# A gated delta stage whose gate factors move from VectorE to ScalarE, and a routed stage whose blank rows are written in long pieces

## The reference, cut to what matters

```python
def step(S, inp):                       # layer 0, once per token; 16 heads of 64x64
    qt, kt, vt, at, bt = inp
    err = jnp.einsum('bhij,bhj->bhi', S, kt) - vt
    S = at[..., None] * S - bt[..., None, None] * (err[..., None] * kt[:, :, None, :])
    o = jnp.einsum('bhij,bhj->bhi', S, qt)
    return (S, o)
...
logits = (xf @ Wr + br) / TAU           # layer 3, routed experts
top_val, top_idx = jax.lax.top_k(logits, 2)
h = jnp.einsum('nd,edh->enh', xf, We1) + be1[:, None, :]
```

## Time and profile before

| | us |
|---|---|
| median of 3 runs (lowest, highest) | 3070.89 (3068.77, 3072.56) |
| the profiled execution, its own time | 3057.68 |
| its span | 3055.9 |
| busy in the span: PE, DVE, ACT, POOL | 2376.6, 2214.9, 1278.8, 272.4 |
| granted TensorE clock, mean share of full speed | 0.857 |

### The profile page before, as it was taken

One profiled execution on the slowest core, in us unless ns is written; L12 is line 12 of the kernel. 1 busy time (PEld: TensorE's weight loads), 2 busy tenths in 40 slices (PEclk: granted clock), 3 DMA queues, 4 the chain that ended last, 5 costly groups with the idle time before them and its releaser, 6 DMA issues. The chain is left out here.

```text
span 3055.9 us, 65022 instructions
## 1 busy us (share of the span) xinstructions
PE 2376.6 (78%) x25365; PEld 1619.7 (53%) x25365; DVE 2214.9 (72%) x4056; ACT 1278.8 (42%) x2862; POOL 272.4 (9%) x280
## 2 busy tenths in 40 slices
PE   6677777777777777769947999999767766778677
PEld 5667666666666666643314666666322221222366
DVE  6999999999999999960034877777255657665465
ACT  3333333333333333332225777776411132556334
POOL 0000000000000000000031010100022311110242
PEclk9777787877777878789977999999978887999888
DMA  4111101111111111011018999995000001110421
GB/s 173 30 30 30 30 22 24 30 30 30 30 30 30 30 30 30 16 39 27 0 50 228 250 229 244 234 239 137 35 0 0 0 23 56 41 41 24 156 68 62
DMA packets 200028, 214.43 MB, mean 70 GB/s; under 512 B 32150, under 2 KB 185766, under 8 KB 194310
## 3 DMA queue, kind: packets, MB, share of 16 engines
q1 hardware_dynamic: 197353, 205.39, 25.7%
q0 software_dynamic: 2400, 4.95, 0.5%
HBM read 138.16 MB, written 74.74 MB: 70 GB/s over the span
## 5 line engine op out<-in xcount | busy, mean ns | idle before, releaser
L1274 DVE TENSOR_REDUCE ra_top<-ps 128x1 f32<-128x512 f32 x256 | 161.6, 684 | 96.0 <-PE ps L1078 95.7
L2557 DVE TENSOR_REDUCE dl_ZO<-dl_XP 128x64 f32<-128x128 f32 (+6 forms) x448 | 219.7, 490 | 15.4
L2553 DVE TENSOR_TENSOR dl_XP<-dl_ZO,dl_G 128x64 f32<-128x64 f32 (+6 forms) x448 | 194.6, 434 | 15.4
L1928 DVE TENSOR_TENSOR ps<-ps,da_window 128x192 f32<-128x192 f32 (+1 forms) x256 | 101.3, 396 | 122.3 <-PE ps L1657 117.9
L1772 ACT ACTIVATE da_AB<-ps 128x384 f32<-128x384 f32 x256 | 124.8, 492 | 146.9 <-PE ps L1634 143.2
L1195 ACT ACTIVATE ra_PT<-ps 128x512 f32<-128x512 f32 x256 | 137.0, 597 | 115.6 <-PE ps L1097 115.5
L1782 ACT ACTIVATE da_E<-ps,da_top 128x512 f32<-128x512 f32 x256 | 176.3, 688 | 17.3 <-DVE da_top L1931 16.9
L1931 DVE TENSOR_REDUCE da_top<-ps 128x1 f32<-128x512 f32 x256 | 177.0, 691 | 8.8
L1664 PE MATMUL ps<-ident,da_E 128*128 128x128 f32 x1024 | 169.0, 288 | 1.3 <-ACT da_E L1782 1.2
L1473 POOL MEMSET da_K<- 32x4096 f32 x2 | 7.1, 3574 | 1559.8 <-POOLq L82 1559.8
L2163 PE MATMUL ps<-X,dl_taps_q 128*128 (+1 forms) x1088 | 144.8, 299 | 0.0
(11 more groups left out here) (397 smaller groups left out, 5668.2 us busy)
## 6 DMA issues: line engine op xcount, KB each, us to landing
da_bands<-da_AB SPq DMA_DIRECT2D x128, 384.0 KB, 3.8
dl_Abc<-dl_ends SPq DMA_DIRECT2D x64, 512.0 KB, 6.2
da_window<-da_bands SPq DMA_DIRECT2D x128, 192.0 KB, 4.4
da_across<-da_bands SPq DMA_DIRECT2D x128, 192.0 KB, 4.5
da_parts<-da_split SPq DMA_DIRECT2D x64, 96.0 KB, 3.4
rf_We<-in_rf_We SPq DMA_DIRECT2D x1, 4608.0 KB, 23.2
da_K<-da_parts SPq DMA_DIRECT2D x16, 256.0 KB
da_Q<-da_parts SPq DMA_DIRECT2D x16, 256.0 KB
```

Source lines behind the costliest of these rows:

```text
L1274: eng.tensor_reduce(top[:, m % 2, u:u + 1], ps[:, score_bank(UNITS * m + u), :], AXX, ALU.max, negate=True).then_inc(s["maxima"], 1)
L2553: link(eng.tensor_tensor(XP[:, :, :, SB - t:], seen.unsqueeze(1).to_broadcast([P, 2, I, t + 1]), G[:, x:x + 2, keys][:, ::-1, :].unsqueeze ...
L2557: link(eng.tensor_reduce(ZO[:, to:to + 1 + (2 * I - 1) * CH:CH].rearrange("p (k i) -> p k i", k=2), XP[:, :, :, SB - 1 - t:], AXX, ALU.add))
```

## The change

In the delta stage DVE now turns gates and values densely into the two halves of `dl_Y` (named `decays` and `values`), for all but the first pass. ACT copies the gates from there into `dl_aT` (512 columns), copies the half's 16 columns of `beta` and of minus `beta` into `dl_beta_now`, and writes `dl_bv` token by token: 16 activations of 32 columns, each scaled by its column of `beta_now`. When DVE has scanned `dl_F`, ACT writes `dl_FB` in the same way, 16 activations more. DVE's two products per half are gone. A new semaphore `laid` counts ACT's four steps per half; DVE's scan waits for the first, and `begin`, which overwrites `dl_Y`, for the last. In the second half `dl_FB` comes behind `later_products` on ACT. The first pass keeps the old way (`prepare_first`).

In the routed stage the fill of `rf_slots` is the same 2.8 MB, seen as 128 rows of 5590 floats in place of 5504 rows of 130, and the bias columns are laid out on the host with the experts side by side, so that the view in line 712 has step one.

```diff
-        yield [..., (s["filled"], [(slots, d["rf_blank"])]), (s["experts_loaded"], large)]
+        yield [..., (s["filled"], [(slots.rearrange("(p j) x -> p (j x)", p=P), d["rf_blank"].rearrange("(p j) x -> p (j x)", p=P))]), (s["experts_loaded"], large)]
...
-            own_bias = bias[:, 0:E * 2 * HR].rearrange("p (e m) -> p m e", e=E)
+            own_bias = bias[:, 0:E * 2 * HR].rearrange("p (m e) -> p m e", e=E)
...
+        values, decays = Y[:, 0:CH, :], Y[:, CH:, :]
...
+            def lay_out(m, e):
+                at = 2 * m + e + 1
+                eng.wait_ge(s["transposed"], 3 * at - 2)
+                eng.activation(aT[:, e, :, :, 1:].rearrange("p i u t -> p u t i"), decays[:, :, :].rearrange("p (u t) i -> p u t i", t=SB), ACT.Copy)\
+                   .then_inc(s["laid"], 1)
+                for sign in range(2):
+                    eng.activation(beta_now[:, sign, :], half_of(beta, m, e), ACT.Copy, scale=1.0 - 2.0 * sign).then_inc(s["laid"], 1)
+                eng.wait_ge(s["transposed"], 3 * at - 1)
+                eng.wait_ge(s["laid"], 4 * at - 9)
+                for t in range(CH):
+                    ins = eng.activation(bv[:, e, :, t], values[:, t, :], ACT.Copy, scale=beta_now[:, 0, t:t + 1])
+                ins.then_inc(s["laid"], 1)
+
+            def scale_decays(m, e):
+                at = 2 * m + e + 1
+                eng.wait_ge(s["transposed"], 3 * at)
+                for t in range(CH):
+                    ins = eng.activation(FB[:, e, :, t // SB, t % SB], F[:, e, :, t // SB, t % SB], ACT.Copy, scale=beta_now[:, 1, t:t + 1])
+                ins.then_inc(s["prep"], 1)
...
                 boundary(n, 0)
+                lay_out(n + 1, 0)
+                scale_decays(n + 1, 0)
                 evacuate(n + 1, AV, 6)
...
                 boundary(n, 1)
+                lay_out(n + 1, 1)
                 later_products(n + 1)
+                scale_decays(n + 1, 1)
...
+                eng.transpose(decays[:, :, :], aN[:, span, :]).then_inc(s["transposed"], 1)
+                eng.transpose(values[:, :, :], vN[:, span, :]).then_inc(s["transposed"], 1)
...
+            def prepare(m, e):
+                eng.wait_ge(s["laid"], 4 * (2 * m + e + 1) - 11)
+                accumulate(m, e)
...
             def begin(n, e):
                 j = 2 * n + e
                 at = BEGUN * j
+                eng.wait_ge(s["laid"], 4 * j)
                 eng.wait_ge(s["y"], 6 * j + 4)
```

More of the change, by code:

```diff
@@ L451, in routed_ffn @@
         ps = c.ps
-        yield [(s["loaded"], pairs), (s["filled"], [(slots, d["rf_blank"])]), (s["experts_loaded"], large)]
+        yield [(s["loaded"], pairs), (s["filled"], [(slots.rearrange("(p j) x -> p (j x)", p=P), d["rf_blank"].rearrange("(p j) x -> p (j x)", p=P))]), (s["experts_loaded"], large)]
         block = c.block(ctx)
@@ L2045, in delta_attention @@
              "gate", "var", "log", "scaled", "normed", "wo", "wo_copied", "transposed", "prefix", "prep", "whole",
-             "abc", "begun", "halves")
+             "abc", "begun", "halves", "laid")
     s = {n: c.nc.alloc_semaphore(name="dl_" + n) for n in names}
@@ L2078, in delta_attention @@
         bv = c.sb("dl_bv", [P, 2, I, CH], ctx)
+        beta_now = c.sb("dl_beta_now", [P, 2, CH], ctx)
         Y = c.sb("dl_Y", [P, XC, I], ctx)
+        values, decays = Y[:, 0:CH, :], Y[:, CH:, :]
         XP = c.sb("dl_XP", [P, 2, I, SB + 1], ctx)
@@ L2466, in turn_values, with accumulate, prepare_first @@
                 eng.wait_ge(s["evac"], m * PROJ + AV)
+                eng.transpose(decays[:, :, :], aN[:, span, :]).then_inc(s["transposed"], 1)
+                eng.transpose(values[:, :, :], vN[:, span, :]).then_inc(s["transposed"], 1)
+            def accumulate(m, e):
+                at = 2 * m + e + 1
+                flat = "p i u t -> p (i u t)"
+                eng.tensor_tensor_scan(F[:, e, :, :, :].rearrange(flat), aT[:, e, :, :, :].rearrange(flat), first_one[:, :, :, :].rearrange(flat),
+                                       0.0, ALU.mult, ALU.add).then_inc(s["transposed"], 1)
+                eng.wait_ge(s["transposed"], 3 * at)
+                eng.tensor_tensor(whole[:, e, :], F[:, e, :, 0, SB], F[:, e, :, 1, SB], ALU.mult).then_inc(s["prefix"], 1)
+            def prepare(m, e):
+                eng.wait_ge(s["laid"], 4 * (2 * m + e + 1) - 11)
+                accumulate(m, e)
+            def prepare_first(e):
+                span = slice(e * CH, (e + 1) * CH)
+                eng.wait_ge(s["evac"], AV)
                 eng.transpose(aT[:, e, :, :, 1:].rearrange("p i u t -> p u t i"),
@@ L2469, in turn_values @@
                 eng.transpose(bv[:, e, :, :].rearrange("p i t -> p t i"), vN[:, span, :]).then_inc(s["transposed"], 1)
[L2471 to L2480, removed]
+                eng.wait_ge(s["transposed"], 3 * e + 2)
+                accumulate(0, e)
+                eng.tensor_tensor(bv[:, e, :, :], bv[:, e, :, :], half_of(beta, 0, e).unsqueeze(1).to_broadcast([P, I, CH]), ALU.mult)
                 eng.tensor_tensor(FB[:, e, :, :, :], F[:, e, :, :, 0:SB],
-                                  half_of(nbeta, m, e).rearrange("p (u t) -> p u t", t=SB).unsqueeze(1).to_broadcast([P, I, 2, SB]), ALU.mult)\
+                                  half_of(nbeta, 0, e).rearrange("p (u t) -> p u t", t=SB).unsqueeze(1).to_broadcast([P, I, 2, SB]), ALU.mult)\
                    .then_inc(s["prep"], 1)
@@ L2623, in _ @@
             for e in range(2):
-                turn_values(0, e)
-                prepare(0, e)
+                prepare_first(e)
             empty_state()
@@ L2707, in laid_out @@
         "rf_order": np.broadcast_to(100.0 - np.arange(E, dtype=np.float32), (P, E)),
-        "rf_be2": np.concatenate([g[L3 + "be2"], np.zeros((P - E, P), np.float32)]), "rf_bias": columns(*(g[L3 + n] for n in ("be1", "bs1", "bs2"))),
+        "rf_be2": np.concatenate([g[L3 + "be2"], np.zeros((P - E, P), np.float32)]), "rf_bias": columns(g[L3 + "be1"].reshape(E, -1, P).transpose(1, 0, 2), g[L3 + "bs1"], g[L3 + "bs2"]),
         "rf_Ws1": g[L3 + "Ws1"].reshape(P, -1, P), "rf_Ws2": rows_in(g[L3 + "Ws2"]),
```

## The result

| | before | changed |
|---|---|---|
| median, us | 3070.8 (3068.8 to 3072.6, 4 runs) | 3111.7 (3106.4 to 3114.1, 4 runs) |
| ratio to before | | 1.0136 [1.012, 1.0151] |
| span of the profiled execution, us | 3055.9 | 3111.6 |
| DVE busy, us | 2214.9 | 2160.3 |
| delta stage ends on DVE at, us | 1362.7 | 1405.3 |

The changed kernel is 40.9 us slower, more than twice the 18 that were forecast, and inside the range (3068 to 3118). A stage ends here where DVE's first operation of the layer norm behind it starts. The two profiled spans differ by 55.7 us, of which the delta stage has 42.6 and the routed stage 11.9; the profiled execution of the kernel before lies 13 us under the median of its runs, so the medians differ by less.

A forecast was written before the change was run, and what follows sets the result against it. DVE was taken to bound the delta stage. Half 0 at -16.5, the first pass +1.0, half 1 +35.5 and the routed stage -2.3 gave +18, so 3089 us against a median of 3070.9; range 3068 to 3118.

The forecast's parts named there:

- Its sign: Whole kernel: slower, with chance 0.8 of more than 0.2%; within 0.2% 0.1, faster 0.1.
- the stall that it was built on: Delta stage, end of half 1: DVE waits for ACT's dl_FB before begin's first product, 3.8 us each, 16 times.
- What bounds the kernel: Delta stage: DVE bounds it, busy 1205.9 of 1260 us; what leaves its queue, and waits put there, count in full.
- What leaves DVE: Delta half ends: the two products leave 1.1 us; denser turns gain nothing in half 0, 0.55 in half 1.
- ACT's price: Delta stage on ACT: 16 activations of 32 columns take n = 3.5 us, with bounds 2.7 and 6.7.
- Half 1: Delta stage: dl_FB comes behind dl_GX on ACT; DVE stalls nearly four us where 1.65 was saved, losing 2.2.
- The first pass's +1.0 us: Delta stage, first pass, half 0: without a norm DVE arrives 2.5 us earlier and waits for dl_FB, +1.0.
- The routed stage: Line 712 drops from 5.71 to 3.4 us, freeing POOL's held scatter: about 2.3 us gained; filling the blanks gains nothing.
- The sum: Whole kernel: half 0 -16.5, first pass +1.0, half 1 +35.5, routed stage -2.3, together +18 us.

The follow-up runs named there:

- e5_pad8: The changed kernel with the memset of dl_W cut into 9 pieces, 8 instructions more ahead of DVE's pass loop: 3017.2 us against 3055.6 for the kernel before, ratio 0.9874.
- e2_routed_only: The kernel before with only the routed edits (long blank pieces, bias with step one), delta stage as before: 3056.5 us, ratio 1.0003 to the kernel before.
- e12_wait_next: The changed kernel with 1 instruction more ahead of the loop and begin waiting for one more set of dl_FB: 3079.4 us against 3057.6 for the kernel before, ratio 1.0076.
- e6_after_again: The unaltered changed kernel timed again, beside the kernel before on the same chip: 3098.5 us against 3055.6, ratio 1.0139.

## Why the prediction was wrong

Its sign was right and its range held the result, both by luck: the stall that it was built on did not exist, and a larger one that it had no term for took its place.

- **What bounds the kernel: right.** DVE's queue sets the delta stage. What left it came back in full, 39.0 us at the stage's end in `e5_pad8` (1362.7 to 1323.7). In the profiles of the other four kernels without stalls and without the extra work the stage ended at 1319.4 to 1321.5 us, and in a second profile with the old delta stage, `e2_routed_only`, at 1358.8, so 39 is good to some 4 us.
- **What leaves DVE: right in size.** The dense turns take 0.67 each (forecast 0.71), `dl_whole` follows the scan directly. Measured from the turn into `dl_W` (line 2549 before, 2586 now) to the reader of `dl_FB`, as the mean over 15 passes (half 0 without the first pass, which has no norm), half 0 went from 13.74 us to 12.70 in `e5_pad8`, a gain of 1.04 (forecast 1.1), and half 1 from 13.75 to 12.46, 1.29 (forecast 1.65 ahead of its loss). In half 0 the turns' gain became a wait for PE's state update, 0.65 in the pass shown, as forecast. That is 2.33 a pass, 35 us in 15 passes, of the 39.
- **ACT's price: near.** n, the time of 16 activations, was 3.96 us (starts 0.24 apart) against 3.5, and 3.53 for `dl_bv` (0.21 apart). By the forecast's own sum half a microsecond would have been 7 us; where nobody waits it is nothing.
- **Half 1: the step that failed.** The forecast let DVE wait for the set of `dl_FB` that stands behind `dl_GX`: it took the last writer of `dl_FB` ahead of its reader in the stream for the one that it waits for. The value says otherwise: `begin` of half j waits for `prep` to reach j + 1. `prep` counts sets of `dl_FB`, and ACT writes them a pass ahead (`scale_decays(n + 1, e)`). At the end of half 1 of pass n, `begin` is for half 0 of pass n + 1, whose set ACT wrote half a pass earlier. In the trace the reader starts 0.07 us before the writer that it was said to wait for. `e12_wait_next`, which waits for j + 2, measures what the forecast computed: 4.2 us where 3.8 was forecast, and +22 in all where +18 was. The arithmetic of the wait was right, and the wait did not exist. The forecast had said what would prove it wrong, a wait of half 1 under 2.5 us, but named two causes for that case, the price of n and the order behind `dl_GX`, and neither was the cause: n was 3.96, and `dl_FB` does stand behind `dl_GX`.
- **The first pass's +1.0 us** rested on the same dependency. From the first turn into `dl_W` to the third the changed kernel took 75.67 us, before it was 78.44: a gain of 2.8. In `e12_wait_next`, which has the dependency, that first wait is 1.92.
- **What the forecast did not have at all:** 14 jumps back at 5 to 7.5 us. The change took two products from each of the two halves that are prepared ahead of the loop, four instructions, and put one more wait into each of the two `begin` there: two instructions fewer in all, and the loop began to touch a fourth block. No rival was about the place of the code, though both numbers, how many instructions stand ahead of the loop and how many in it, can be counted before a kernel runs.
- **The routed stage: right.** Line 712 took 3.38 us (forecast 3.4), the scatter beside it 3.12 ("near 3"), the stage 2.3 less in `e2_routed_only` (forecast 2.3), 1.7 less on the means of all profiles but the one of 204.8. The inference of the Trainium skill's "SBUF — State Buffer", "Who interferes with whom", that generating descriptors does not suffer from a product with two SBUF inputs, by which this edit is worth nothing, did not hold here: with the product at 5.71 us and at 3.38 the scatter took 5.45 and 3.12, and both times ended 0.84 us after it.
- **The sum:** -39.0 at the stage's end, +83.9 of stalls and -2.3 make +42.6, against 40.9 measured. The forecast's +18 lay between a kernel that gains 38 and one that loses 41. It had the terms of the gain, but set against them a wait that was not there, and it had no term for the loss.

**The version that beats both** is the changed kernel with a few instructions more ahead of DVE's loop: 3017.2 against 3055.6 of the kernel before and 3098.5 of the changed one. One is enough (3012.8 in a single execution), but one leaves it next to the boundary.

Open is what held ACT and DVE 12 us longer in the routed stage of the changed kernel's first profile. There DVE was idle for 19.0 us in 37 pieces ahead of line 740 with no releaser named, against 0.3 in `e6_after_again`; it did not come again in any other profile.

## What to carry to other kernels

Read which count a wait names and which step of the loop raises it to that, and not which writer stands ahead in the stream; with work prepared a pass ahead the two differ. When an edit changes the number of instructions in or ahead of a loop, count them on each engine, and look afterwards at the packets of the instruction queue and at idle "issue" time at the jump back. A few instructions of next to no work ahead of the loop are the cheapest test of that, and settle it before anyone looks for a reason in the work itself.

## What the runs showed of the hardware

A loop of 259 instructions on DVE ran without a fetch for 14 jumps (`e5_pad8`) when it touched three blocks of 128, and fetched five packets of 8 KB in each pass when it touched four, with a stall of 5.1 to 7.5 us at each jump. That is 81 us of the changed kernel's time; with the old loop of 264 instructions, moved, the stalls were 7.1 us a jump, 100 in all. ACT's loop went from 89 to 166 instructions, and no such stall shows on ACT. The Trainium skill, "Runtime: NRT & Kernel Launch", section "Instruction fetch mechanics", says that a branch taken to a place outside the engine's window of instructions stalls until its block is fetched; the stalls at the jump agree. It gives most engines 512 instructions in two blocks of 256. By that the stalls would be back at the same place after 256 instructions; here they were back after 128, with none at 1, 2, 8 or 64.

A second finding is the price of a stepped read on ACT: the activations into `dl_FB`, which read `dl_F` with a step, start 0.24 us apart, those into `dl_bv`, which read densely and write with the same step, 0.21: 0.43 us more in sixteen.
